# Cross attention with a fused output: output projection turned round, 512 columns moving

## The chip, the cores and the metric

The kernel runs on one core of a Trainium2 chip. The metric is the device time of one execution in microseconds; a change is judged by the times of several runs of the kernel before and the kernel after.

## What is computed

For each of 32 batches there are 512 tokens of 640 channels (x) and 77 context tokens of 1,024 channels, all fp32. What of the reference matters for the output (the object, others and ip branches take part with empty contexts, since there are just 77 context tokens, and add nothing):

```python
q = _heads(hidden_states @ to_q_w)                      # 20 heads of 32 channels
h_txt = _sdpa(q, _heads(ehs_txt @ to_k_w), _heads(ehs_txt @ to_v_w))
out = _merge(h_txt) + ...
out = out @ to_out_w + to_out_b
out = (out + residual) / RESCALE                        # residual = x, RESCALE = 1
```

## The kernel before

There are two stages. `project_context` makes keys and values of all context tokens (scratch in DRAM) and splits the weights into a high and a low fp32r part; it takes the first 325 us or so. `attend` then goes through the 32 batches and is the rest.

A batch has five steps g = 0 to 4, one for each group of four heads (128 channels). The order on each engine is written out by hand in the tables `TENSOR`, `SCALAR`, `VECTOR` and `POOL` (lines 67 to 86), one string for a step; the SyncE queue is written in its own body (lines 518 to 536). The letters:

- TensorE: S is the scores of the step (32 small matmuls, L750). Q0 to Q4 is the projection of q for the next step (15 matmuls of 512 columns, L735: five channel chunks, three products of high and low parts each). V is probabilities times values for the step two before (8 matmuls, L762). O and P are the output projection of the batch before and of the one before that (L776). Its unit is a half tile: 128 tokens by 320 channels, 15 matmuls with attention output o_t as weights and wo moving in 320 columns. There are eight a batch, k = 0 to 7.
- VectorE: M takes the maxima of the scores (L638), R the reciprocals of the sums (L644), T turns the probabilities (L654), Q copies q out of its bank (L661), W makes the low part of o_t (L665), Y turns x of the next batch (L671) and X makes its low part (L676). O and P add the output bank to the tile `x_bias` (L684).
- ScalarE: S0 to S3 are the exponentials (16 pairs of instructions, L595), X the high part of turned x (L608), V the high part of o_t (L602). D and E issue loads of x for turning (L582), R issues loads of x by rows into `x_bias` (L587).
- GpSimd: N normalises the probabilities (L562), C adds the bias to `x_bias` (L557).
- SyncE: in each step it loads v, reads back the turned probabilities of the step before from scratch (L508), stores finished output tiles (L496: one tile of 128 tokens, 320 KB, in rows of 2,560 B), and writes the turned probabilities of this step (L500). The load of k is in step 0.

x is turned in squares of 32 x 32: it is loaded in four quarters of 160 channels each, in runs of 640 B, and VectorE's transpose within 32 partitions does the rest. The channels of turned x thus come in a permuted order, and wq is loaded in the same order. Turned x (`x_turned`) has one buffer, the output bank `fill_bank` has two.

In the last batch there is no next x to turn and no q to project in step 4. What is left of the output projection (P5, P6, P7 of batch 30 and all eight of batch 31) stands behind the loop (lines 798 to 804), between and after the last two V.

Of the kernel before, what the change touches and what calls it, by code (L numbers as in the profile page):

```python
# [19 lines left out]
F32, F32R = mybir.dt.float32, mybir.dt.float32r  # L20
# [42 lines left out]
def orders(*steps):  # L63
# [3 lines left out]
TENSOR = orders("S Q0 Q1 Q2 Q3 Q4 P5 V",  # L67
# [4 lines left out]
SCALAR = orders("S0 S1 S2 S3 D1 V",  # L72
                "S0 S1 S2 S3 D2 D3 V",
                "S0 S1 S2 S3 R0 V",
                "S0 S1 S2 S3 R1 R2 X0 X1 X2 X3 X4 V",
                "S0 S1 S2 S3 R3 E0 V")
VECTOR = orders("M W R0 Q R1 T0 R2 T1 R3 T2 P5 T3",
# [30 lines left out]
def cross_attention(nc, x, ctx, wq, wk, wv, wo, bias, out):  # L108
# [3 lines left out]
    with ExitStack() as stack:  # L112
# [13 lines left out]
        x_rows = x.rearrange("b (t p) c -> b p t c", p=P)  # L126
        project_context(nc, ctx, wq, wk, wv, wo, kept, k_scratch, v_scratch, x_v, x_loaded)
        attend(nc, x_v, x_rows, bias, out, kept, k_scratch, v_scratch, p_scratch, x_loaded)


def project_context(nc, ctx, wq, wk, wv, wo, kept, k_scratch, v_scratch, x_v, x_loaded):

    with ExitStack() as stack:  # L133
# [29 lines left out]
        WK_CHUNKS, WKV_CHUNKS = KC, 2 * KC  # L163

# [135 lines left out]
        def _(dve):  # L300
            def split_weights(which):
                for n in which:
                    _, dst, k = chunks[n]
                    dve.wait_ge(w_high, n + 1)
                    nc.vector.tensor_tensor(dst[:, 1, k, :], stage[:, n % WSLOTS, :], dst[:, 0, k, :].bitcast(F32),  # L305
# [84 lines left out]
def attend(nc, x_v, x_rows, bias, out, kept, k_scratch, v_scratch, p_scratch, x_loaded):  # L390

    with ExitStack() as stack:
# [432 lines left out]
```

## Time and profile before

| | us |
|---|---|
| median of 3 runs | 1845.81 (1843.40 to 1849.78) |
| profiled execution, its own time | 1846.19 |
| its span | 1844.5 |
| TensorE busy in the span | 1796.0 (97%) |
| VectorE busy | 1167.8 (63%) |
| ScalarE busy | 1054.0 (57%) |
| GpSimd busy | 689.8 (37%) |
| the core's DMA engines, mean rate | 217 GB/s |

The profile is one execution. Busy time of an engine is the union of its instructions; weight loads of TensorE are counted by themselves. The granted clock of TensorE is given as a share of 2.4 GHz; its lower level is 1.2 GHz. In a timeline or in the chain, consecutive instructions of one line are merged, with their count behind an x; the figure in brackets is idle time before the first, with what ended it.

### The profile page before, as it was taken

How to read it: one execution, taken by the hardware profiler on the slowest of the kernel's cores; microseconds unless marked ns; L12 is line 12 of the kernel's file. 1: busy time of each engine (PE TensorE's matmuls, PEld its weight loads, DVE VectorE, ACT ScalarE, POOL GpSimd, SP SyncE). 2: the span in 40 equal slices, each digit the busy share in tenths (PEclk: the TensorE clock that was granted, in tenths of full speed). 3: DMA queues.
4: the chain of work that ended last, by engine and by line, in shares of the span. 5: the costliest groups of instructions: out<-in, count | busy, mean ns of one | idle time of the engine just before them, and what ended most of it. 6: DMA issues, size and time to landing. Idle time of an engine off the chain costs nothing.

```text
span 1844.5 us, 41902 instructions
## 1 busy us (share of the span) xinstructions
PE 1796.0 (97%) x14960; PEld 1508.3 (82%) x14960; DVE 1167.8 (63%) x2402; ACT 1054.0 (57%) x5597; POOL 689.8 (37%) x865
## 2 busy tenths in 40 slices
PE   8999998689999999999999999999999999999997
PEld 7999998468888888888888888888888888888886
DVE  3201010577777777777777777777777777777762
ACT  4312111476666666666666666666666666666661
POOL 1111111244444444444444444444444444444441
PEclk9999999799999999999999999999999999999998
DMA  7422110588989989989898998988989989998973
GB/s 264 136 85 86 63 44 33 143 227 250 252 247 247 252 249 250 249 250 252 246 251 251 249 250 247 253 248 248 250 251 249 250 249 251 246 254 246 253 217 125
DMA packets 271397, 399.36 MB, mean 217 GB/s; under 512 B 41088, under 2 KB 119024, under 8 KB 271200
## 3 DMA queue, kind: packets, MB, share of 16 engines
q1 hardware_dynamic: 183008, 301.62, 56.1%
q10 hardware_dynamic: 83904, 82.59, 18.5%
q0 software_dynamic: 4288, 12.62, 1.9%
q8 instruction: 111, 1.82, 0.4%
q14 instruction: 86, 0.70, 0.1%
HBM read 216.37 MB, written 180.39 MB: 215 GB/s over the span
## 4 chain that ended last, share of the span: by engine, by line
PE 78%; DVE 1%; ACT 1%; DMA 0%; POOL 0%; issue 0%; SPq 0%; ACTq 0%; DVEq 0%
PE p_bank L735 31%; PE p_bank L776 31%; PE p_scores L750 9%; PE p_bank L762 8%; ACT probs L595 1%; DVE negmax L638 0%; POOL probs L562 0%; DMA probs_t<-p_scratch 0%; DVE turned L654 0%; DMA p_scratch<-turned 0%; DVE x_raw L671 0%; DVE x_t L676 0%; DVE q_t L661 0%; DVE rsum L644 0%; DVE x_bias L684 0%
## 5 line engine op out<-in xcount | busy, mean ns | idle before, releaser
L595 ACT ACTIVATE probs<-p_scores,negmax 128x77 f32<-128x77 f32 x2560 | 787.8, 361 | 332.0 <-DVE negmax L638 332.0
L562 POOL TENSOR_TENSOR probs<-probs,rsum 128x308 f32<-128x308 f32 x640 | 446.5, 700 | 844.4 <-DVE rsum L644 844.3
L595 ACT ACTIVATION_READ_ACCUMULATOR probs<-p_scores,negmax 128x1 f32 x2560 | 622.1, 243 | 0.0
L735 PE MATMUL p_bank<-x_t,wq_split 128*128 128x512 f32 x2400 | 598.9, 401 | 15.8 <-DVE x_t L676 15.8
L776 PE MATMUL p_bank<-wo_split,o_t 128*128 128x320 f32 x3840 | 599.4, 310 | 0.6 <-DVE x_bias L684 0.6
L776 PEld LDWEIGHTS p_bank<-wo_split,o_t 128*128 128x128 f32 x3840 | 578.4, 189 | 17.4 <-issue 2.5
L735 PEld LDWEIGHTS p_bank<-x_t,wq_split 128*128 128x128 f32 x2400 | 445.1, 190 | 116.8 <-DVE x_t L676 17.0
L654 DVE STREAM_TRANSPOSE turned<-probs 128x384 f32<-128x384 f32 x640 | 356.8, 558 | 29.3 <-POOL probs L562 29.0
L638 DVE TENSOR_REDUCE negmax<-p_scores 128x16 f32<-128x1232 f32 x160 | 227.7, 1423 | 86.4 <-PE p_scores L750 86.4
L750 PEld LDWEIGHTS p_scores<-k_sb,q_t 32*128 32x128 f32 x5120 | 157.5, 186 | 146.9 <-issue 146.9
L644 DVE RECIPROCAL rsum<-sums 128x4 f32<-128x4 f32 x640 | 111.1, 174 | 187.6 <-ACT probs L595 183.3
L602 ACT ACTIVATE o_t<-p_bank 128x512 fp32r<-128x512 f32 x160 | 98.5, 615 | 180.7 <-PE p_bank L762 180.7
L557 POOL TENSOR_TENSOR x_bias<-x_bias,bias_all 128x640 f32<-128x640 f32 x128 | 196.4, 1555 | 0.0
L750 PE MATMUL p_scores<-k_sb,q_t 32*128 32x77 f32 x5120 | 181.0, 277 | 13.9 <-ACT probs L595 12.4
L762 PE MATMUL p_bank<-probs_t,v_sb 77*32 77x512 f32 x1280 | 171.3, 607 | 7.1 <-DMA probs_t<-p_scratch 7.1
L311 DVE TENSOR_TENSOR ctx_t<-p_bank,ctx_t 128x512 fp32r<-128x512 f32 (+1 forms) x40 | 26.9, 672 | 224.9 <-ACT ctx_t L264 224.9
L356 PE MATMUL p_bank<-ctx_t,wk_split 128*128 128x256 f32 (+1 forms) x1200 | 156.3, 288 | 2.2 <-DVE wk_split L305 2.2
L356 PEld LDWEIGHTS p_bank<-ctx_t,wk_split 128*128 128x128 f32 x1200 | 148.7, 194 | 2.9 <-DVE wk_split L305 2.6
L661 DVE COPY q_t<-p_bank 128x512 f32<-128x512 f32 x160 | 109.3, 683 | 61.3 <-PE p_bank L735 61.3
L671 DVE STREAM_TRANSPOSE x_raw<-x_raw 128x512 f32<-128x512 f32 x160 | 108.5, 680 | 54.8 <-PEq L133 54.0
L370 PE MATMUL p_bank<-wv_split,ctx_t 128*128 128x320 f32 (+1 forms) x960 | 142.4, 309 | 0.0
L370 PEld LDWEIGHTS p_bank<-wv_split,ctx_t 128*128 128x128 f32 (+1 forms) x960 | 139.0, 184 | 1.9 <-DVE wv_split L305 0.2
(28 smaller groups left out, 634.2 us busy)
## 6 DMA issues: line engine op xcount, KB each, us to landing
p_scratch<-turned SPq DMA_DIRECT2D x160, 768.0 KB, 6.8
probs_t<-p_scratch SPq DMA_DIRECT2D x320, 256.0 KB
x_bias<-in_x ACTq DMA_DIRECT2D x128, 320.0 KB, 3.5
out<-x_bias SPq DMA_DIRECT2D x128, 320.0 KB, 5.6
x_raw<-in_x ACTq DMA_DIRECT2D x124, 320.0 KB, 5.5
probs_t<-p_scratch SPq DMA_DIRECT2D x160, 104.0 KB
ctx_raw<-in_ctx SPq DMA_DIRECT2D x19, 512.0 KB, 4.6
k_sb<-k_scratch SPq DMA_DIRECT2D x32, 192.5 KB, 6.1
```

The source lines that it names most:

```text
L356: last = nc.tensor.matmul(k_bank[slot][:, 0:tokens], wk_s[:, a, k, m * P:(m + 1) * P], ctx_t[parity][:, b, k, 0:tokens], start=n == 0, sto ...
L370: last = nc.tensor.matmul(v_bank[u % 2][0:rows, 0:HALF], ctx_t[parity][:, a, k, t0:t0 + rows], wv_s[:, b, k, hf * HALF:(hf + 1) * HALF], s ...
L557: nc.gpsimd.tensor_tensor(x_bias[:, parity, t, :], x_bias[:, parity, t, :], bias_all[:, :], ALU.add).then_inc(x_bias_ready, 1)
L562: nc.gpsimd.tensor_tensor(heads_of(t), heads_of(t), rsum[:, slot, t, :].unsqueeze(2).to_broadcast([P, HG, N_TXT]), ALU.mult).then_inc(prob ...
L595: last = nc.scalar.activation(heads_of(t)[:, h, :], s_bank[:, h, t * N_TXT:(t + 1) * N_TXT], ACT.Exp, bias=negmax[:, slot, t, h:h + 1], ac ...
L638: nc.vector.tensor_reduce(negmax[:, slot, :, :], s_bank[:, :, 0:QT * N_TXT].rearrange("p h (t k) -> p t h k", k=N_TXT), AX.X, ALU.max, neg ...
L644: nc.vector.reciprocal(rsum[:, slot, t, :], sums[:, slot, t, :]).then_inc(rsum_ready, 1)
L654: nc.vector.transpose(turned[slot][:, :, :, t, :].rearrange("p k h q -> p h k q"), squares_of(t)).then_inc(probs_turned, 1)
L735: last = nc.tensor.matmul(q_bank[:, :], wq_s[:, w, c, g * P:(g + 1) * P], x_t[:, a, c, :], start=c == 0 and i == 0, stop=c == CC - 1 and i ...
L750: last = nc.tensor.matmul(s_bank[:, h, t * N_TXT:(t + 1) * N_TXT], q_t[slot][rows, t * P:(t + 1) * P], k_sb[parity][rows, g, :], start=Tru ...
L762: last = nc.tensor.matmul(pv_bank[h * HD:(h + 1) * HD, :], v_sb[:, g, h * HD:(h + 1) * HD], probs_t[slot][:, :, h, :], start=True, stop=True)
L776: last = nc.tensor.matmul(to_bank[:, 0:HALF], o_t[parity][:, o, c, t * P:(t + 1) * P], wo_s[:, w, c, hf * HALF:(hf + 1) * HALF], start=c = ...
```

## The change

- The output projection takes wo as weights and moves 512 columns of o_t. Its unit becomes a chunk of 128 output channels by all 512 tokens of the batch, 15 matmuls; there are five a batch, k = 0 to 4, one in each step. wo's output channels are put in the order of turned x (`staged`, `split_part`).
- The second loading of x (`x_bias`, L587) and the bias adds on GpSimd (L557) are gone. VectorE joins bank, turned x and the bias, now a column of one value for each partition, in one `scalar_tensor_tensor`, in place into turned x, which gets three buffers.
- VectorE turns each joined chunk back (`turn_output`, Z in the table: five a batch, in steps 0 to 2 two batches later) into `out_blocks`, which has one buffer.
- The output is stored by quarters of 160 channels, in runs of 640 B. All four stores of a batch wait for its five turns; in the loop two stand in step 2 and two in step 3.
- The bias is loaded by four small loads, values of 4 B, one for each 32 partitions.
- Loads and turns of x are a step earlier than before. Behind the loop stand P3 and P4 of batch 30, the five chunks of batch 31, and their adds and turns.

```diff
-TENSOR = orders("S Q0 Q1 Q2 Q3 Q4 P5 V",
-                "S Q0 Q1 Q2 Q3 Q4 P6 P7 V",
+TENSOR = orders("S Q0 Q1 Q2 Q3 Q4 P3 V",
+                "S Q0 Q1 Q2 Q3 Q4 P4 V",
                 "S Q0 Q1 Q2 Q3 Q4 O0 V",
-                "S Q0 Q1 Q2 Q3 Q4 O1 O2 V",
-                "S O3 Q0 Q1 Q2 Q3 Q4 O4 V")
-SCALAR = orders("S0 S1 S2 S3 D1 V",
-                "S0 S1 S2 S3 D2 D3 V",
-                "S0 S1 S2 S3 R0 V",
-                "S0 S1 S2 S3 R1 R2 X0 X1 X2 X3 X4 V",
-                "S0 S1 S2 S3 R3 E0 V")
-VECTOR = orders("M W R0 Q R1 T0 R2 T1 R3 T2 P5 T3",
-                "M W R0 Q R1 T0 R2 T1 R3 T2 P6 T3 P7",
-                "M W Y0 R0 Q R1 T0 R2 T1 Y1 R3 T2 O0 T3 Y2",
-                "M W Y3 R0 Q R1 T0 Y4 R2 T1 R3 T2 O1 T3 X0 X1 O2",
-                "M X2 X3 X4 W R0 R1 T0 O3 R2 T1 Q R3 T2 T3 O4")
-POOL = orders("N0 N1 N2 N3 C0 C1",
-              "N0 N1 N2 N3 C2 C3",
-              "N0 N1 N2 N3",
-              "N0 N1 N2 N3",
-              "N0 N1 N2 N3")
-
-HALVES = 2 * QT
-CREDIT = 16
+                "S Q0 Q1 Q2 Q3 Q4 O1 V",
+                "S O2 Q0 Q1 Q2 Q3 Q4 V")
+SCALAR = orders("S0 S1 S2 S3 D3 V",
+                "S0 S1 S2 S3 V",
+                "S0 S1 S2 S3 V",
+                "S0 S1 S2 S3 E0 X0 X1 X2 X3 X4 V",
+                "S0 S1 S2 S3 E1 E2 V")
+VECTOR = orders("M W Z0 R0 Q R1 T0 Z1 R2 T1 R3 T2 Z2 T3 P3",
+                "M W Z3 R0 Q R1 T0 Y0 R2 T1 R3 T2 Y1 T3 P4",
+                "M W Z4 R0 Q R1 T0 Y2 R2 T1 R3 T2 Y3 T3 O0",
+                "M W Y4 R0 Q R1 T0 R2 T1 R3 T2 T3 X0 X1 O1",
+                "M X2 X3 X4 W R0 R1 T0 O2 R2 T1 Q R3 T2 T3")
+POOL = orders(*["N0 N1 N2 N3"] * CC)
+
+XT = 3
...
+        def staged(n):
+
+            chunk = stage[:, n % WSLOTS, :]
+            return chunk.rearrange("p (i k s) -> p k i s", i=P // SQ, s=SQ) if chunks[n][0] is wo else chunk
+
+        def split_part(n, part):
+
+            dram, dst, k = chunks[n]
+            chunk = dst[:, part, k, :]
+            return chunk.rearrange("p (k i s) -> p k i s", i=P // SQ, s=SQ) if dram is wo else chunk
...
-                    _, dst, k = chunks[n]
                     act.wait_ge(w_loaded[n % WSLOTS], DMA * loads_by(n))
-                    nc.scalar.activation(dst[:, 0, k, :], stage[:, n % WSLOTS, :], ACT.Copy).then_inc(w_high, 1)
+                    nc.scalar.activation(split_part(n, 0), staged(n), ACT.Copy).then_inc(w_high, 1)
...
-        bias_all = sbuf("bias_all", [P, C])
+        bias_t = sbuf("bias_t", [P, CC])
         x_blocks = x_raw[:, 0, :, :]
-        x_turned = x_raw[:, 1, :, :].rearrange("p n c -> p (n c)").rearrange("p (c s) -> p c s", s=S)
-        x_bias = sbuf("x_bias", [P, 2, QT, C])
+        x_turned = [x_raw[:, 1, :, :].rearrange("p n c -> p (n c)").rearrange("p (c s) -> p c s", s=S)]
+        x_turned += [sbuf(f"x_turned{i}", [P, CC, S]) for i in range(1, XT)]
+        out_blocks = sbuf("out_blocks", [P, S // SQ, CQ])
...
-            def store_out(b, parity, t):
-                sp.wait_ge(out_added, HALVES * b + 2 * t + 2 + CREDIT)
-                sp.dma_start(out_v[b][t], x_bias[:, parity, t, :]).then_inc(out_stored[t], DMA)
+            def store_out(b, i):
+                sp.wait_ge(out_turned, CC * (b + 1))
+                sp.dma_start(out_v[b][i], out_blocks[i * SQ:(i + 1) * SQ, :, :]).then_inc(out_stored, DMA)
 
             def write_probs(n, slot):
                 sp.wait_ge(probs_turned, QT * (n + 1))
@@ -509,8 +510,10 @@
                                  p_scratch[slot, k].rearrange("(i p) c -> p i c", p=SQ)[0:rows])\
                       .then_inc(probs_read[slot], DMA)
 
-            sp.dma_start(bias_all[:, :], bias.rearrange("(a n) -> a n", a=1).broadcast_to([P, C]))\
-              .then_inc(bias_loaded, DMA)
+            for i in range(P // SQ):
+                sp.dma_start(bias_t[i * SQ:(i + 1) * SQ, :], bias.rearrange("(i k s) -> i s k", i=P // SQ, s=SQ)[i],
+                             allow_slow_non_contiguous=True)\
+                  .then_inc(bias_loaded, DMA)
...
-                    for kind, k in TENSOR[(g - 1) % CC]:
-                        if kind == "O" and k % 2 == 1 and g > 0 and age > 0:
-                            store_out(b - 1, 1 - parity, k // 2)
-                        if kind == "O" and k % 2 == 1 and g == 0 and age > 1 or kind == "P" and k % 2 == 1 and age > 1:
-                            store_out(b - 2, parity, k // 2)
+                    if g in (2, 3) and age > 1:
+                        store_out(b - 2, 2 * g - 4)
+                        store_out(b - 2, 2 * g - 3)
...
-            store_out(B - 2, (B - 2) % 2, 1)
             sp.wait_ge(pv_done, CC * B - 2)
             read_probs(CC * B - 1, (CC * B - 1) % 2)
-            for t in (2, 3):
-                store_out(B - 2, (B - 2) % 2, t)
-            for t in range(QT):
-                store_out(B - 1, (B - 1) % 2, t)
-            for t in range(QT):
-                sp.wait_ge(out_stored[t], DMA * B)
+            for b in (B - 2, B - 1):
+                for i in range(P // SQ):
+                    store_out(b, i)
+            sp.wait_ge(out_stored, DMA * (P // SQ) * B)
...
-            pool.wait_ge(bias_loaded, DMA)
-
-            def add_bias(b, parity, t):
-
-                pool.wait_ge(x_bias_loaded[t], DMA * (b + 1))
-                nc.gpsimd.tensor_tensor(x_bias[:, parity, t, :], x_bias[:, parity, t, :], bias_all[:, :],
-                                        ALU.add).then_inc(x_bias_ready, 1)
...
-            def load_x_bias(b, parity, t):
-                if b > 1:
-                    act.wait_ge(out_stored[t], DMA * (b - 1))
-                act.dma_start(x_bias[:, parity, t, :], x_rows[b][:, t, :]).then_inc(x_bias_loaded[t], DMA)
...
-                nc.vector.transpose(x_turned[:, c, :].rearrange("p (n q) -> p n q", q=SQ),
+                nc.vector.transpose(x_turned[b % XT][:, c, :].rearrange("p (n q) -> p n q", q=SQ),
...
-            def add_output(b, k, parity, from_bank):
-                t, hf = k // 2, k % 2
-                dve.wait_ge(out_done, HALVES * b + k + 1)
-                dve.wait_ge(x_bias_ready, QT * b + t + 1)
-                tile = x_bias[:, parity, t, hf * HALF:(hf + 1) * HALF]
-                nc.vector.tensor_tensor(tile, from_bank[:, 0:HALF], tile, ALU.add).then_inc(out_added, 1)
-
-            dve.sem_inc(out_added, CREDIT)
+            def add_output(b, k):
+                n = CC * b + k
+                if n == 0:
+                    dve.wait_ge(bias_loaded, DMA * (P // SQ))
+                dve.wait_ge(out_done, n + 1)
+                tile = x_turned[b % XT][:, k, :]
+                nc.vector.scalar_tensor_tensor(tile, fill_bank[n % 2][:, :], bias_t[:, k:k + 1], tile,
+                                               ALU.add, ALU.add).then_inc(out_added, 1)
+
+            def turn_output(b, k):
+                dve.wait_ge(out_added, CC * b + k + 1)
+                if b > 0:
+                    dve.wait_ge(out_stored, DMA * (P // SQ) * b)
+                nc.vector.transpose(out_blocks[:, :, k * SQ:(k + 1) * SQ],
+                                    x_turned[b % XT][:, k, :].rearrange("p (n q) -> p n q", q=SQ))\
+                  .then_inc(out_turned, 1)
...
-            add_output(B - 2, 5, (B - 2) % 2, fill_bank[1])
+            for k in range(3):
+                turn_output(B - 2, k)
+            add_output(B - 2, 3)
+            turn_output(B - 2, 3)
             ot_low_part(B - 1, CC - 2, (B - 1) % 2)
-            for k in (6, 7):
-                add_output(B - 2, k, (B - 2) % 2, fill_bank[k % 2])
+            add_output(B - 2, 4)
+            turn_output(B - 2, 4)
             ot_low_part(B - 1, CC - 1, (B - 1) % 2)
-            for k in range(HALVES):
-                add_output(B - 1, k, (B - 1) % 2, fill_bank[k % 2])
+            for k in range(CC):
+                add_output(B - 1, k)
+                turn_output(B - 1, k)
...
-            def project_out(b, k, parity, to_bank):
-                if k >= 2:
-                    pe.wait_ge(out_added, HALVES * b + k - 1 + CREDIT)
-                else:
-                    pe.wait_ge(out_added, HALVES * b + CREDIT)
-                t, hf = k // 2, k % 2
+            def project_out(b, k, parity):
+                n = CC * b + k
+                if n >= 2:
+                    pe.wait_ge(out_added, n - 1)
                 for c in range(CC):
                     if k == 0 and c in (0, CC - 1):
                         pe.wait_ge(ot_ready, CC * b + (CC - 1 if c == 0 else CC))
                     for i, (o, w) in enumerate(PASSES):
-                        last = nc.tensor.matmul(to_bank[:, 0:HALF], o_t[parity][:, o, c, t * P:(t + 1) * P],
-                                                wo_s[:, w, c, hf * HALF:(hf + 1) * HALF],
-                                                start=c == 0 and i == 0, stop=c == CC - 1 and i == 2)
+                        last = nc.tensor.matmul(fill_bank[n % 2][:, :], wo_s[:, w, c, k * P:(k + 1) * P],
+                                                o_t[parity][:, o, c, :], start=c == 0 and i == 0,
+                                                stop=c == CC - 1 and i == 2)
...
-            project_out(B - 2, 5, (B - 2) % 2, fill_bank[1])
+            project_out(B - 2, 3, (B - 2) % 2)
             sum_values(B - 1, CC - 1, (CC * B - 1) % 2)
-            for k in (6, 7):
-                project_out(B - 2, k, (B - 2) % 2, fill_bank[k % 2])
-            for k in range(HALVES):
-                project_out(B - 1, k, (B - 1) % 2, fill_bank[k % 2])
+            project_out(B - 2, 4, (B - 2) % 2)
+            for k in range(CC):
+                project_out(B - 1, k, (B - 1) % 2)
```

## Rows read from the trace of the kernel before

**Rows 1.** Window: us, busy (instructions) of PE, PEld, DVE, ACT, POOL; clock, DMA share, GB/s.
```profile
700.00:1700.00 1000.00, 1000.00 (x8588) 811.08 (x8587) 758.24 (x1581) 661.53 (x3687) 435.77 (x522) 1.00 0.90 250
```

**Rows 2.** Chain of waits, steady batches: start us, us, what. Step 4, then parts of steps 0 and 1.
```profile
415.13 1.06 PE p_scores L750 x32
416.19 2.39 PE p_bank L776 x15
418.58 3.43 PE p_bank L735 x15
422.01 2.20 PE p_bank L776 x15
424.21 1.00 PE p_bank L762 x8
...
426.26 3.63 PE p_bank L735 x15
...
437.78 4.40 PE p_bank L776 x30
```

**Rows 3.** Groups of instructions by line, middle stretch: busy us, mean ns | idle before.
```profile
L671 DVE STREAM_TRANSPOSE x_raw<-x_raw 128x512 f32<-128x512 f32 x109 | 74.2, 680 | 0.0
```

**Rows 4.** Timelines of TensorE and of VectorE in one batch: start us, us, what [idle before].
```profile
1207.80 1.13 PE L750 MATMUL p_scores<-k_sb,q_t 32*128 32x77 f32 x32
...
1212.41 2.36 PE L776 MATMUL p_bank<-wo_split,o_t 128*128 128x320 f32 x15
...
1203.83 0.58 DVE L654 STREAM_TRANSPOSE turned<-probs 128x384 f32<-128x384 f32 x1 [0.50 <-POOL probs L562]
...
1205.25 0.65 DVE L661 COPY q_t<-p_bank 128x512 f32<-128x512 f32 x1
...
1209.00 1.44 DVE L638 TENSOR_REDUCE negmax<-p_scores 128x16 f32<-128x1232 f32 x1 [1.25 <-PE p_scores L750]
...
1212.61 0.69 DVE L661 COPY q_t<-p_bank 128x512 f32<-128x512 f32 x1 [0.59 <-PE p_bank L735]
...
1235.60 1.40 DVE L638 TENSOR_REDUCE negmax<-p_scores 128x16 f32<-128x1232 f32 x1
...
1243.08 0.58 DVE L654 STREAM_TRANSPOSE turned<-probs 128x384 f32<-128x384 f32 x1
...
1244.75 0.48 DVE L684 TENSOR_TENSOR x_bias<-p_bank,x_bias 128x320 f32<-128x320 f32 x1
1245.15 1.43 DVE L638 TENSOR_REDUCE negmax<-p_scores 128x16 f32<-128x1232 f32 x1
...
1248.30 0.69 DVE L665 TENSOR_TENSOR o_t<-p_bank,o_t 128x512 fp32r<-128x512 f32 x1
1248.90 0.48 DVE L644 RECIPROCAL rsum<-sums 128x4 f32<-128x4 f32 x2
1249.88 0.58 DVE L654 STREAM_TRANSPOSE turned<-probs 128x384 f32<-128x384 f32 x1 [0.50 <-POOL probs L562]
```

**Rows 5.** Timelines of VectorE and TensorE at the start of the second stage.
```profile
336.34 0.69 DVE L661 COPY q_t<-p_bank 128x512 f32<-128x512 f32 x1 [4.00 <-PE p_bank L735]
...
337.13 1.13 PE L750 MATMUL p_scores<-k_sb,q_t 32*128 32x77 f32 x32 [0.83 <-issue]
```

**Rows 6.** The end of the program: TensorE's timeline, the chain of waits, a window.
```profile
1807.77 1.93 PE L762 MATMUL p_bank<-probs_t,v_sb 77*32 77x512 f32 x8 [4.80 <-DMA probs_t<-p_scratch]
1809.63 4.25 PE L776 MATMUL p_bank<-wo_split,o_t 128*128 128x320 f32 x15
...
1816.73 6.14 PE p_bank L776 x30
...
1841.35 0.49 DVE x_bias L684
...
1807.00:1816.00 9.00, 6.45 (x27) 4.38 (x31) 1.09 (x2) 0.60 (x1) 3.91 (x3) 0.63 0.71 233
```

**Rows 7.** ScalarE's queue at the start of the second stage: four loads of x issued.
```profile
329.40 2.02 ACTq L582 DMA_DIRECT2D x_raw<-in_x  x4
```

More of the change, by code:

```diff
@@ L125, in cross_attention @@
         x_v = x.rearrange("b (n q) (i c) -> b i q n c", q=SQ, i=P // SQ)
-        x_rows = x.rearrange("b (t p) c -> b p t c", p=P)
+        out_v = out.rearrange("b (n q) (i c) -> b i q n c", q=SQ, i=P // SQ)
         project_context(nc, ctx, wq, wk, wv, wo, kept, k_scratch, v_scratch, x_v, x_loaded)
-        attend(nc, x_v, x_rows, bias, out, kept, k_scratch, v_scratch, p_scratch, x_loaded)
+        attend(nc, x_v, bias, out_v, kept, k_scratch, v_scratch, p_scratch, x_loaded)
 def project_context(nc, ctx, wq, wk, wv, wo, kept, k_scratch, v_scratch, x_v, x_loaded):
@@ L302, in split_weights @@
                 for n in which:
-                    _, dst, k = chunks[n]
                     dve.wait_ge(w_high, n + 1)
-                    nc.vector.tensor_tensor(dst[:, 1, k, :], stage[:, n % WSLOTS, :], dst[:, 0, k, :].bitcast(F32),
+                    nc.vector.tensor_tensor(split_part(n, 1), staged(n), split_part(n, 0).bitcast(F32),
                                             ALU.subtract).then_inc(w_split, 1)
@@ L387, in _, with attend @@
             blocks(pe, body)
-def attend(nc, x_v, x_rows, bias, out, kept, k_scratch, v_scratch, p_scratch, x_loaded):
+def attend(nc, x_v, bias, out_v, kept, k_scratch, v_scratch, p_scratch, x_loaded):
     with ExitStack() as stack:
@@ L430, in attend @@
         xt_turned, xt_high, xt_ready = sem("xt_turned"), sem("xt_high"), sem("xt_ready")
-        out_done, out_added = sem("out_done"), sem("out_added")
-        x_bias_ready = sem("x_bias_ready")
-        x_bias_loaded = [sem(f"x_bias_loaded{t}") for t in range(QT)]
-        out_stored = [sem(f"out_stored{t}") for t in range(QT)]
-        out_v = out.rearrange("b (t p) c -> b t p c", p=P)
+        out_done, out_added, out_turned, out_stored = (sem("out_done"), sem("out_added"), sem("out_turned"),
+                                                       sem("out_stored"))
         def heads_of(t):
@@ L465, in steps @@
                 for kind, k in order[g]:
-                    left_out = (kind in "OC" and age == 0 or kind == "P" and age < 2 or kind in "XY" and last
+                    left_out = (kind == "O" and age == 0 or kind in "PZ" and age < 2 or kind in "XY" and last
                                 or kind == "V" and age == 0 and g < 2 or kind == "W" and age == 0 and g < 3
@@ L567, in body @@
                 for g, slot, kind, k in steps(POOL, b, parity, age, last):
-                    if kind == "N":
-                        normalise(b, g, slot, k)
-                    elif kind == "C":
-                        add_bias(b - 1, 1 - parity, k)
+                    normalise(b, g, slot, k)
             batches(body)
-            for t in range(QT):
-                add_bias(B - 1, (B - 1) % 2, t)
         @block.scalar
@@ L607, in xt_high_part @@
                     act.wait_ge(q_done, CC * b)
-                nc.scalar.activation(x_t[:, 0, c, :], x_turned[:, c, :], ACT.Copy).then_inc(xt_high, 1)
+                nc.scalar.activation(x_t[:, 0, c, :], x_turned[b % XT][:, c, :], ACT.Copy).then_inc(xt_high, 1)
             for c in range(CC):
@@ L622, in body @@
                         xt_high_part(b + 1, k)
-                    elif kind == "R":
-                        load_x_bias(b, parity, k)
                     elif kind == "D" and 0 < b < B - 1:
```

12 lines of the change are left out of this document (7 added, 5 removed).

## The prediction

> **What bounds the kernel now.** I read the busy time by stretch first: over 1,000 us in the middle TensorE is busy for all 1,000, at the full granted clock of 2.4 GHz, VectorE for 758, ScalarE for 662 [rows 1]. Then the chain of waits shows what that means in time: in the middle it is nothing but blocks of matmuls, end to end [rows 2]. So a batch costs what its blocks cost, and VectorE, ScalarE, GpSimd and the transfers matter only if one of them becomes late.
>
> The blocks [rows 2]: scores (S) 1.06, query projection (Q) 3.63 behind scores and 3.43 behind a projection, one half tile of the output projection (O) 2.20, or 2.39 behind scores, two of them 4.40, values (V) 1.00. A batch is 5 x 1.06 + 4 x 3.63 + 3.43 + 7 x 2.20 + 2.39 + 5 x 1.00 = 46.04 us. Its five steps are uneven: with one O 7.89 us, with two 10.09 or 10.08.
>
> **The change part by part.**
>
> *Output matmuls.* Removed are 120 matmuls of 320 columns per batch (2.20 / 15 = 147 ns each), added are 75 of 512 columns. The columns are the same 38,400. The new form has exactly the shape of the Q matmul (128x128 weights, 512 moving columns of the same type), which costs 3.43 / 15 = 229 ns. So an output chunk costs 3.43, and 3.63 directly behind scores, as Q does. There are five a batch, one a step, of which one is behind scores (step 4: S O2 Q V): 4 x 3.43 + 3.63 = 17.35 in place of 7 x 2.20 + 2.39 = 17.79. Gain 0.44 us a batch; new batch 45.6, and every step 9.12. The gain is only the share per matmul that is not columns; bounds from the same rows: nothing, if the new block ran at the per-column price of the old (0.458 ns x 512 x 15 = 3.52, sum 17.8), and 0.44.
> The Trainium skill (TensorE: Matmul & The Clock Gate, Back-to-back issue gap) gives columns / 2.4 plus about 2.5 ns per matmul. By it 45 fewer matmuls would be worth only 0.11 us a batch, an estimate from that page. The trace disagrees at both sizes, 147 ns against its 136 and 229 against its 216, and the measurement decides.
>
> *How much of it arrives.* Batches 2 to 30 are full: 29 x 0.44 = 12.8. In batch 1 only steps 2 to 4 hold output work: 27.4 for 28.1, gain 0.7. In batch 31 the next landmark is the scores of step 3, after steps with one, two and one O: 25.9 before, 3 x 9.12 = 27.4 after, loss 1.5. At that landmark the new kernel is 12.0 us ahead.
>
> *Does VectorE keep up?* Per batch it loses 8 adds of 320 (0.40 from start to start) and gains 5 joined adds of 512 and 5 transposes back. The trace has no scalar_tensor_tensor. Nearest is the subtraction from PSUM of 512 elements, 0.60 from start to start; I take that, since it too reads one PSUM and one SBUF operand. Bounds: 0.40 (the 320 add) and 1.4, the maxima over 1232 elements [rows 4]. The transposes back I take as those of x, 0.68 [rows 3], 0.67 from start to start. VectorE gains 5 x 0.60 + 5 x 0.67 - 3.2 = 3.2 us a batch, on 46.04 x 0.758 = 34.9 busy; it ends at about 38 of 45.6. The cover is its idle time, but position matters. In steps 0 to 2 the work behind the last probs transpose ends at about 10.1 after the step's scores start, and the next maxima can start at 9.12 + 1.20 = 10.32: fits. The tight place is step 3 to 4, in the terms of [rows 4] (all counted from a step's scores): maxima start at 1.20; last transpose T3 7.48 later (1235.60 to 1243.08), 8.68; then X0, X1 and the add take 2.07 until the next maxima, 0.20 more with 512 elements: 10.95, that is 1.83 in step 4. From the maxima to T0 4.73 (1245.15 to 1249.88): 6.56. From T0 to the copy of q 1.42 (1203.83 to 1205.25) and 0.20 more: VectorE is there at 8.18. The block Q now ends at 1.06 + 3.63 + 3.43 = 8.12, since O4 no longer stands behind it, and the copy starts 0.20 after (1212.41 to 1212.61): 8.32. The copy takes 0.69 and the scores start 0.10 after it, as at the start of the stage (copy 336.34 + 0.69, scores 337.13 [rows 5]): 9.11, where V ends at 9.12. So no stall, with a reserve of 0.15 us on VectorE's side and none on the copy's. Queued behind that wait are the scores of the next batch's step 0, and all that follows on TensorE. I take 0 and keep 0.3 a batch (9 us) in the range.
>
> *Exponentials.* A step must leave room for maxima, 16 exponentials and the release of the scores' banks. That fits in 7.89 today with TensorE never idle [rows 1]; the new steps are 9.12, and the maxima of step 4, 0.6 late, use half of the new room. Nothing.
>
> *GpSimd and ScalarE.* The bias adds (1.55 us each on GpSimd) and the second loading of x leave; both lay beside the matmuls. Worth 0. The last load of x moves from step 1 to step 0 and the turns of x from step 2 to step 1, so their distance stays. Worth 0.
>
> *Transfers.* 1.3 MB a batch is no longer read; the 1.3 MB stored go in runs of 640 B instead of 2,560. On SyncE two stores now stand in steps 2 and 3 between the read-back of probs and the next write of probs: at some 0.45 us each they finish about when T3 does, delaying that write by 0.1; V uses it two steps later. Worth 0. The single out_blocks buffer makes the first turn back wait for the stores of the batch before, which were issued three steps earlier. Worth 0.
>
> *Start.* Four bias loads stand ahead of k on SyncE instead of one: 3 x 0.4 = 1.2 us later, and k is wanted only at 337.13. Their 4-byte runs have no row; between 0 and 3 us, I take 0.3, because the q copy ends last there today. (The Trainium skill, DMA: Bandwidth & Descriptors, head table, asks for 512 B and more per run for full rate. No row here shows runs so short, and the bias is 640 of them, once.)
>
> *End.* V of step 3 in the last batch starts a fixed time after that step's scores [rows 6], so it is 12.0 early. From there (1807.77) to the last matmul's end (1841.3) it was 33.55. After: V 1.86 (the granted clock is 0.63 on average from 1807 to 1816, after 4.8 us idle); chunk 3 at the lower clock 4.25 x 512 / 320 = 6.8, or less if the clock returns inside it; then V of step 4 waits for a subtraction that stands on VectorE behind the add and the new turn: 0.68 + 0.67 + 0.68, 2.1 with the handovers; V 1.06; six chunks 20.6, and 1.7 for clock again, what the first two halves lost today (6.14 against 4.40). Sum 34.1, so 0.5 lost; bounds -3 and +3. Then today one add (0.49) and one store of 320 KB: 3.2 from the last matmul to the span's end. After: add 0.68, turn 0.67, and all four stores of the batch, since the quarters cut across channels and wait for the last turn. Issuing four takes 2.0 [rows 7], landing 2.3 more, or about 5.5 if 1.3 MB flows at the 250 GB/s of the middle: 5.6 to 7.2, I take 6.5, 3.3 more than today.
>
> **Sum.** -12.0 + 0.5 + 3.3 + 0.3 = -7.9. The profiled execution took 1846.2 (span 1844.5), the median is 1845.8: 1846.2 - 7.9 - 0.4 = 1838.
>
> **The rivals.**
> *A: the copy of q becomes late* (step 4). For it: two new long adds and three x subtractions stand on that path, with 0.15 us to spare; against: VectorE has 7 us of slack a batch. With adds of 0.75 from start to start the path is 0.3 longer, the stall 0.15 to 0.3, a loss of 5 to 9: about 1845, no change.
> *B: slower.* The same place, with the joined add much longer than the subtraction (the extra per-partition operand), or the transposes back slower than those of x: a stall of 0.26 us a batch (adds of 0.81) uses up the 7.9, and from 0.43 (adds of 0.89) the kernel is measurably slower than today. At 1.1 us both adds lengthen the path by 1.0, the stall is 0.85 x 30 = 25, time 1863; the other bound, 1.4, would cost more. Against: each 512-element kind in the trace costs 0.68 or less.
> *C: hardly any gain in the matmuls*, if the new block costs its columns at the old price (3.52) or o_t moves slower than x does: then the end decides, and the time is 1838 + 0.44 x 30 = 1851, or 1845 at half of it. The Q rows speak against it. (The page named above would put it there: 0.11 a batch makes about 1848.)
> *D: the end goes well and nothing stalls*, the clock returns early in the first chunk of the tail and the stores land in 5 us: 1834.
>
> **How the numbers follow.** A comparison of this kernel can tell some 0.3%, 5.5 us: faster means below 1840.3, slower above 1851.3. Forecast 45% and D 12%, both faster for nearly all their width; A 23%, C 8%, both same; B 12%. Some of the forecast's width reaches above 1840.3. Faster 0.54, same 0.33, slower 0.13. The range 1832 to 1849 leaves out B and the far ends.
>
> **What would show it.** In the chain: blocks of 3.43 for the output, steps of 9.12, a batch of 45.6; scores of step 0 with no wait for the copy of q (a wait there is A). VectorE: joined add near 0.68, with B from 0.95. In the tail: V of step 4 released by VectorE, not by a transfer, and 6.5 us from the last matmul to the end. A batch above 46.0 or TensorE idle in the middle would make the forecast wrong.

## The result: slower by 0.8%

| | before | after |
|---|---|---|
| median, us (5 runs each) | 1844.56 (1843.40 to 1849.78) | 1859.48 (1859.31 to 1861.81) |
| ratio, 95% interval | | 1.0081 (1.0070 to 1.0093) |
| profiled execution, its span | 1846.19, 1844.5 | 1859.48, 1857.8 |
| TensorE / VectorE / GpSimd busy | 97 / 63 / 37% | 97 / 68 / 27% |
| weight loads busy | 82% | 74% |

The forecast was 1838 in a range to 1849. The time lies 21 us above it, on the other side of the kernel before.

The window of the middle stretch answers to [rows 1], with the same columns: TensorE is as full as before, at the full clock (1.00). No wait took the place of the work removed.

```profile
700.00:1700.00 1000.00, 999.98 (x7559) 723.00 (x7559) 818.45 (x1620) 658.82 (x3671) 302.58 (x434) 1.00 0.84 219
```

The chain of waits answers to [rows 2]. In order: scores of step 0 of batch 2; step 4 and the start of step 0 in the middle; scores of step 0 of batch 31. L729 is the query projection, L768 the output projection.

```profile
424.94 1.12 PE p_scores L744 x32
...
925.24 1.06 PE p_scores L744 x32
926.30 3.69 PE p_bank L768 x15
929.99 3.50 PE p_bank L729 x15
933.49 0.99 PE p_bank L756 x8
934.48 1.12 PE p_scores L744 x32
935.60 3.69 PE p_bank L729 x15
939.29 3.50 PE p_bank L768 x15
...
1768.18 1.12 PE p_scores L744 x32
```

From the first of these rows to the last are 29 batches in 1343.24 us, 46.32 each; before they took 46.04, and 45.60 was forecast. The output block takes 3.49 (3.69 behind scores) where 3.43 was forecast. The surprise is the query block, which the change does not touch in any line: 3.70 behind scores and 3.50 behind the output block, where it took 3.63 and 3.43 in [rows 2]. All 512-column matmuls are some 4 ns slower each.

The new instructions of VectorE by line (busy us, mean ns | idle before), and the stretch before the critical copy of q (the last row). The joined add is longer than the 0.68 taken, 0.72, and 0.63 to 0.66 from start to start.

```profile
L664 DVE SCALAR_TENSOR_TENSOR x_turned<-p_bank,bias_t,x_turned 128x512 f32<-128x512 f32 x70 | 50.1, 716 | 0.0
L671 DVE STREAM_TRANSPOSE out_blocks<-x_turned 128x512 f32<-128x512 f32 x70 | 48.2, 689 | 0.0
```

```profile
1018.92 0.74 DVE L664 SCALAR_TENSOR_TENSOR x_turned<-p_bank,bias_t,x_turned 128x512 f32<-128x512 f32 x1
...
1024.81 0.71 DVE L664 SCALAR_TENSOR_TENSOR x_turned<-p_bank,bias_t,x_turned 128x512 f32<-128x512 f32 x1
1025.44 0.16 DVE L623 RECIPROCAL rsum<-sums 128x4 f32<-128x4 f32 x1
...
1026.13 0.69 DVE L640 COPY q_t<-p_bank 128x512 f32<-128x512 f32 x1
```

TensorE in the same place, the block Q, the values and the scores of step 0:

```profile
1022.44 3.65 PE L729 MATMUL p_bank<-x_t,wq_split 128*128 128x512 f32 x15
1026.02 1.06 PE L756 MATMUL p_bank<-probs_t,v_sb 77*32 77x512 f32 x8
1027.08 1.13 PE L744 MATMUL p_scores<-k_sb,q_t 32*128 32x77 f32 x32
```

Over the middle stretch this copy starts 0.43 us after the last of its matmuls starts, as the other four copies of a batch do, which all wait for theirs. So it is the block Q that releases it here, and VectorE is there some 0.1 sooner. From the copy's end (1026.82) to the scores are 0.26, where 0.10 was taken, so the scores of step 0 start 1.06 after V, and those of the other steps 1.00.

The end answers to [rows 6]: the scores of step 3 in the chain; TensorE's timeline with both last V, the chunk between them and the last output chunks; VectorE's first turn of the last batch, which waited 5.51 for the stores of the batch before, and its last; then the transfers of the last 9 us (from 1849 to 1858, in 40 slices).

```profile
1795.99 1.11 PE p_scores L744 x32
...
1815.45 1.94 PE L756 MATMUL p_bank<-probs_t,v_sb 77*32 77x512 f32 x8 [4.44 <-DMA probs_t<-p_scratch]
1817.31 4.92 PE L768 MATMUL p_bank<-o_t,wo_split 128*128 128x512 f32 x15
...
1824.44 1.06 PE L756 MATMUL p_bank<-probs_t,v_sb 77*32 77x512 f32 x8 [2.21 <-DVE o_t L644]
...
1840.41 7.26 PE L768 MATMUL p_bank<-o_t,wo_split 128*128 128x512 f32 x30 [0.70 <-DVE x_turned L664]
...
1839.01 0.71 DVE L671 STREAM_TRANSPOSE out_blocks<-x_turned 128x512 f32<-128x512 f32 x1 [5.51 <-DMA out<-out_blocks]
...
1848.50 0.71 DVE L671 STREAM_TRANSPOSE out_blocks<-x_turned 128x512 f32<-128x512 f32 x1
...
GB/s 0 0 0 0 23 188 182 185 188 185 182 182 185 182 182 179 185 174 188 145 171 256 290 259 216 233 196 202 196 185 179 182 179 185 131 31 0 0 0 0
DMA packets 2112, 1.31 MB, mean 146 GB/s; under 512 B 64, under 2 KB 2112, under 8 KB 2112
```

The account in the profiled executions, after minus before, counted to four landmarks: scores of step 3 in batch 31 +9.8 (1786.23 before, 1795.99; forecast -12.0); from there to V of step 3 -2.1 (21.54 before, 19.46; forecast 0); to the last matmul's end -1.3 (33.55 before, 32.2; forecast +0.5); to the end of the span +6.9 (3.2 before, 10.1; forecast +3.3). Sum +13.3, the difference of the spans. The forecast names 0.3 more for the start of the stage. So practically the whole miss is in the first term; the three of the end add up to +3.5, where +3.8 was forecast.

### The profile page after: what moved, and what is told of

The parts are those of the page before. It is cut to its first block, busy times and chain, and to the rows that moved or that the text cites. A ratio compares the mean times of both kernels' runs of the same rounds, so it can differ in the third digit from the quotient of the medians.

```text
span 1857.8 us, 38728 instructions
## 1 busy us (share of the span) xinstructions
PE 1801.6 (97%) x13520; PEld 1381.6 (74%) x13520; DVE 1261.6 (68%) x2466; ACT 1054.8 (57%) x5597; POOL 497.5 (27%) x737
## 4 chain that ended last, share of the span: by engine, by line
PE 78%; DVE 2%; ACT 1%; DMA 1%; POOL 0%; issue 0%; SPq 0%; ACTq 0%; DVEq 0%
PE p_bank L729 31%; PE p_bank L768 30%; PE p_scores L744 9%; PE p_bank L756 8%; ACT probs L576 1%; DVE negmax L617 0%; DMA out<-out_blocks 0%; DVE turned L633 0%; POOL probs L553 0%; DMA p_scratch<-turned 0%; DMA probs_t<-p_scratch 0%; DVE x_t L655 0%; DVE x_raw L650 0%; DVE out_blocks L671 0%; SPq L497 0%
## 5 line engine op out<-in xcount | busy, mean ns | idle before, releaser
L729 PE MATMUL p_bank<-x_t,wq_split 128*128 128x512 f32 x2400 | 607.1, 405 | 15.5 <-DVE x_t L655 15.5
L768 PE MATMUL p_bank<-o_t,wo_split 128*128 128x512 f32 x2400 | 589.7, 397 | 0.7 <-DVE x_turned L664 0.7
L729 PEld LDWEIGHTS p_bank<-x_t,wq_split 128*128 128x128 f32 x2400 | 445.6, 190 | 126.1 <-DVE x_t L655 16.4
L768 PEld LDWEIGHTS p_bank<-o_t,wo_split 128*128 128x128 f32 x2400 | 449.0, 188 | 112.5 <-issue 2.5
L633 DVE STREAM_TRANSPOSE turned<-probs 128x384 f32<-128x384 f32 x640 | 352.5, 551 | 40.0 <-POOL probs L553 39.8
L644 DVE TENSOR_TENSOR o_t<-p_bank,o_t 128x512 fp32r<-128x512 f32 x160 | 108.9, 680 | 0.0
L287 ACT ACTIVATE v_out<-p_bank 128x320 f32<-128x320 f32 (+1 forms) x40 | 17.5, 438 | 122.6 <-PE p_bank L374 119.4
```

Of the source, the lines that this page charges most:

```text
L633: nc.vector.transpose(turned[slot][:, :, :, t, :].rearrange("p k h q -> p h k q"), squares_of(t)).then_inc(probs_turned, 1)
L644: nc.vector.tensor_tensor(o_t[parity][:, 1, g, :], pv_bank[:, :], o_t[parity][:, 0, g, :].bitcast(F32), ALU.subtract).then_inc(ot_ready, 1)
L729: last = nc.tensor.matmul(q_bank[:, :], wq_s[:, w, c, g * P:(g + 1) * P], x_t[:, a, c, :], start=c == 0 and i == 0, stop=c == CC - 1 and i ...
L768: last = nc.tensor.matmul(fill_bank[n % 2][:, :], wo_s[:, w, c, k * P:(k + 1) * P], o_t[parity][:, o, c, :], start=c == 0 and i == 0, stop ...
```

## The experiments

Two numbers decide in most of them. One is the mean time from start to start of the matmuls inside a block (the first of the 14 times of a block left out, 700 to 1,700 us, worked out from the start times in each trace). The other is where the tiles lie in a partition, which follows from the order and sizes of the allocations, each rounded up to 32 B. wq starts at 37,504 and wo at 63,104 in all but two kernels; both leave 128 on division by 512, as do all slices of them that a matmul loads. "Distance" is the rest of the moving tile minus that of the weights, modulo 512. The kernel before was run again with every round (medians 1844.73 to 1846.74), and ratios are to that; where it says one run, there is no interval, but each mean of the 512-column blocks is over some 1,400 matmuls even so.

| kernel | query: distance, ns | output, 512 columns: distance, ns | batch, us |
|---|---|---|---|
| before | 0, 229.5 | (320 columns) 146.4 | 46.04 |
| after | 32, 233.2 | 96, 233.7 | 46.32 |
| a_pad, a_order, a_tail | 64, 229.4 to 229.5 | 128, 232.3 | 45.99 |
| t_swapps, t_swapw | 64, 229.4 | 128, 232.2 to 232.3 | 45.99 |
| a_o64 | 64, 229.8 | 192, 232.9 | 46.07 |
| a_noturn | 32, 233.1 | 96, 233.7 | 46.31 |
| t_swapsb | 128, 232.5 | 64, 229.6 | 45.98 |
| t_low, t_hi0, t_all64 | 0, 228.0 to 228.2 | 0, 227.0 | 45.62 to 45.64 |
| t_best | 0, 228.1 | 0, 227.0 | 45.48 |
| t_mix | 64, 229.2 | 256, 228.3 | 45.74 |
| b_qorder | 0, 229.5 | (320) 146.4 | 46.04 |
| b_shift32 | 32, 233.2 | (320) 146.9 | 46.37 |
| b_shift64 | 64, 229.3 | (320) 146.5 | 46.10 |
| b_high | 64, 229.6 | (320) 146.7 | 46.11 |

**First round: the tiles' places against VectorE's traffic.** The unchanged query block had slowed, so either where x_t lies or what runs beside it had to be the cause. The new bias tile is 20 B per partition and pushes x_t and o_t 32 B off a 64 B boundary.

a_pad:
```diff
-        bias_t = sbuf("bias_t", [P, CC])
+        bias_t = sbuf("bias_t", [P, 16])
```


> The changed kernel with its bias tile widened from 5 to 16 floats per partition (64 B in place of 20), nothing else. In the changed kernel every tile allocated behind the bias, x_t and o_t among them, starts 32 B off a 64 B boundary; here all start on one. Theory 1 (placement): the 512-column matmuls go from 233 ns start to start to 229, a block from 3.50 to 3.43, a batch from 46.3 to 45.6 us, the time from 1859 to about 1838. Theory 2 (VectorE's added reads and writes of SBUF slow TensorE's reads): nothing changes, 1859.

```profile
1308.61 3.64 PE p_bank L729 x15
1312.25 3.48 PE p_bank L768 x15
```

Measured 1850.70 (ratio to before 1.0025, 1.0015 to 1.0034). In the chain (query, output) the query block is back at 3.64, the output block hardly moved: 3.48. Half of the steady loss is gone, the time that theory 1 named is missed by 13 us.

b_shift32, an unused tile behind the bias of the kernel before:
```diff
         bias_all = sbuf("bias_all", [P, C])
+        shift = sbuf("shift", [P, 8])
```


> The kernel before with an unused tile of 32 B per partition behind the bias, so that x_t, o_t and all later tiles start 32 B off a 64 B boundary; wq and wo stay where they were. Theory 1: the query projection, which moves x_t, goes from 229 to 233 ns a matmul, a batch from 46.04 to about 46.4, the time up by 10 us to about 1855; the output projection, which moves wo, stays at 147 if only the moving operand counts. Theory 2: nothing changes, 1845.

```profile
1307.23 3.69 PE p_bank L736 x15
1310.92 2.21 PE p_bank L777 x15
```

Measured 1856.93 (1.0057, 1.0041 to 1.0074), query block 3.69 where it was 3.63, with no other work than before. 32 B of nothing cost 10 us. The output block, where o_t is loaded as weights, stays at 2.21.

b_shift64, the same with `[P, 16]`:

> The kernel before with an unused tile of 64 B per partition at the same place: everything moves, but stays on 64 B boundaries. Theory 1: all as before, query projection 229 ns a matmul, 1845. If it slows here too, it is not the boundary but the distance between tiles. Theory 2: 1845.

One run, 1849.13; query matmuls 229.3. As theory 1 has it, except that the batch is 0.06 longer.

a_noturn, `out_blocks` filled by full transposes in batch 0 only:
```diff
-                nc.vector.transpose(out_blocks[:, :, k * SQ:(k + 1) * SQ],
+                n = S // SQ if b == 0 else 1
+                nc.vector.transpose(out_blocks[:, 0:n, k * SQ:(k + 1) * SQ],
```


> The changed kernel, with the turning back of the output cut to one 32-column square of each chunk from batch 1 on (most of the output is left unturned), waits and order kept. Theory 1: matmuls stay at 233 ns and a batch at 46.3; the time falls only at the end, by 1 to 2 us. Theory 2: VectorE moves about 3 us less a batch, the matmuls fall towards 229 ns, the time by up to 20 us.

```profile
1314.22 3.70 PE p_bank L730 x15
1317.92 3.49 PE p_bank L769 x15
```

One run, 1856.66: both blocks as in the changed kernel, with 2.3 us a batch less busy time on VectorE. Theory 2 falls.

**Second round: why output matmuls stay at 232, and the end.** a_order (in `project_out`, on a_pad):
```diff
-                    for i, (o, w) in enumerate(PASSES):
+                    for i, (w, o) in enumerate(PASSES):
```


> The changed kernel with the 64 B bias tile, and in the output projection the three products of a channel chunk in the order high-high, then wo low with o_t high, then wo high with o_t low: the moving plane stays the same for two matmuls running, as it does in the query projection. With the 64 B tile alone the query block is back at 3.64 but the output block only at 3.48, 232 ns a matmul. Theory 1 (the order of the planes is what is left): output matmuls at 229 to 230, block 3.44, a batch 0.2 us less, 1845. Theory 2 (it is where o_t or wo lies, or that o_t is used at all): unchanged at 232 and 1851.

1851.24 (1.0021, 1.0012 to 1.0031), 232.3 ns: unchanged, the theory falls.

a_o64 (on a_pad, `shift = sbuf("shift", [P, 16])` ahead of o_t):

> The changed kernel with the 64 B bias tile and another 64 B of nothing ahead of o_t, so that o_t leaves the 128 B boundary on which wo also starts and has the offset that x_t has. If the place of o_t within 128 B matters, the output matmuls fall from 232 to 229; if the order of the planes or the tensor itself is the cause, they stay at 232 and the time near 1851.

One run, 1852.30, 232.9 ns: the rest modulo 128 is not it.

b_qorder, the same exchange of loop variables in `project_q` of the kernel before:

> The kernel before with the products of the query projection in the other order, so that the moving plane of x_t changes at nearly every matmul, as o_t's does in the changed kernel. Order theory: query matmuls from 229.5 to about 232, a batch up by 0.2 us, 1851. Place theory: nothing moves, 1845.

One run, 1846.32; 229.5 ns as before. The order of the planes plays no part.

a_tail, on a_pad:
```diff
+                to = x_blocks if b == B - 1 else out_blocks   # no wait for out_stored in the last batch
...
+            ot_low_part(B - 1, CC - 2, (B - 1) % 2)
             add_output(B - 2, 3)
             turn_output(B - 2, 3)
-            ot_low_part(B - 1, CC - 2, (B - 1) % 2)
...
+        PARTS = ((0, 3), (3, CC))                              # stores of the last batch; i = 2, 3 by ScalarE
+            eng.wait_ge(out_turned, CC * (B - 1) + k1)
```


> The changed kernel with the 64 B bias tile and another end: the last batch is turned into the idle half of x_raw instead of waiting for out_blocks, it is stored in two parts (chunks 0 to 2, then 3 and 4), half of the stores issued by ScalarE's queue, and the subtraction that the last V waits for stands ahead of the add and turn of chunk 3. In the kernel with the 64 B tile alone the last matmul ends 35.0 us after V of step 3 starts and the span 10.0 after that. If the end is lost to the store rate and to VectorE's order: 31 to 32 and 6 to 7, the time from 1851 to about 1844. If the stores of 256-byte runs are no faster than those of 640, only the first part is gained: 1847.

```profile
1806.74 1.94 PE L769 MATMUL p_bank<-probs_t,v_sb 77*32 77x512 f32 x8 [4.75 <-DMA probs_t<-p_scratch]
...
1814.39 1.06 PE L769 MATMUL p_bank<-probs_t,v_sb 77*32 77x512 f32 x8 [0.98 <-DMA probs_t<-p_scratch]
...
1837.37 0.71 DVE x_raw L684
```

Measured 1844.29 (0.9987, 0.9977 to 0.9996), 6 to 7 us under a_pad. In TensorE's timeline both last V wait for their transfers and no longer for VectorE; from V of step 3 to the last matmul 29.8 us (35.0 in a_pad), and from there to the span's end (1842.2) 5.6 (10.0). Part of the 35.0 is clock: from 1800 to 1842 the granted clock was 0.84 in the profiled a_pad, 0.92 in the changed kernel and 0.91 here. Against the 32.2 and 10.1 of the changed kernel the new end gives 2.4 and 4.5. These are VectorE's order and the stores; the edits were made together, and no run takes them apart.

The stores of the last batch, from 1830 to 1842.2 in 40 slices, chunks 0 to 2 first, then 3 and 4:

```profile
GB/s 0 0 0 0 0 0 64 172 259 264 277 315 310 281 312 277 47 0 0 0 0 0 0 0 0 0 0 0 0 92 149 241 276 284 229 270 173 5 0 0
DMA packets 4224, 1.31 MB, mean 107 GB/s; under 512 B 4224, under 2 KB 4224, under 8 KB 4224
```

These runs are shorter (384 and 256 B for 640), and the rate is higher, 230 to 315 GB/s for about 185. So it was not the length of the runs that held the rate in the changed kernel.

**Third round: exchange of places**, all on a_tail. t_swapsb allocates o_t where x_t is and x_t where o_t is; t_swapps exchanges the PSUM banks; t_swapw exchanges wq and wo.

> The kernel with the 64 B bias tile and the new end, with o_t allocated in the place of x_t and x_t in the place of o_t. There the query matmuls took 229.4 ns start to start and the output matmuls 232.3. Theory place (high in the partition is slower to read): the two change over, output 229 to 230, query 232. Theory other (banks, weights, or the writers of the tile): they stay as they are.

```profile
1309.93 3.69 PE p_bank L742 x15
1313.62 3.44 PE p_bank L781 x15
```

> The same kernel as a base, with the PSUM banks of query and output projection exchanged (query in the fourth bank, output in the first and third). If the bank written to makes the difference, the output matmuls on the first bank fall to 229 and the query rises to 232; otherwise nothing moves: 229.4 and 232.3, 1844.

> The same kernel as a base, with the places of wq and wo exchanged. If the place of the weights makes the difference, query 232 and output 229; otherwise 229.4 and 232.3, 1844.

One run each: 1843.46, 1842.80, 1843.73. In the first the two kinds change over: query 3.69, output 3.44 (in the chain's rows), 232.5 and 229.6 ns. Exchanging the banks (229.4 and 232.2) or the weights (229.4 and 232.3) does nothing. It is the place of the moving tile; the weights' exchange leaves both at the same rest modulo 512, so it says nothing yet of the distance to them.

**Fourth round: which places.** t_low, on a_tail:
```diff
+        x_t = sbuf("x_t", [P, 2, CC, S], F32R)
+        o_t = [sbuf(f"o_t{i}", [P, 2, CC, S], F32R) for i in range(2)]
         bias_t = sbuf("bias_t", [P, 16])
```


> The kernel with the 64 B bias tile and the new end, with x_t and both o_t allocated first, below 150,144 B of the partition, everything else behind them. Exchanging x_t and o_t exchanged their speeds (232.5 and 229.6 ns). Place theory: both at 229.5 now, a batch from 45.99 to about 45.8, the time from 1844 to about 1838, 0.4% under the kernel before. If only one certain place is fast and not the lower part as such, one of them stays at 232 and the time near 1844.

```profile
1311.01 3.62 PE p_bank L742 x15
1314.64 3.40 PE p_bank L781 x15
...
1336.20 0.99 PE p_bank L769 x8
1337.19 0.15 issue
1337.34 1.13 PE p_scores L757 x32
```

1833.22 (0.9931, 0.9917 to 0.9944), better than its own theory: 227 and 228 ns. Both blocks are under the forecast (3.62 and 3.40). The last three rows show what came with it: V, then 0.15 of waiting, then the scores of step 0.

b_high, x_t allocated last in the kernel before:

> The kernel before, x_t allocated last, from 196,800 B of the partition, on a 64 B boundary as before; o_t, which is loaded as weights here, 20,480 B lower. Place theory: query matmuls from 229.5 to 232.5, a batch 0.22 us longer, 1852. If the effect needs the changed kernel's work around it: 1845.

One run, 1848.08, 229.6 ns. High and no slower: "the lower part is fast" falls. What all kernels up to here fit is the distance.

t_hi0 (on a_tail, padded so that x_t at 119,936 and o_t at 184,960 have distance 0), t_mix (on t_low, x_t 64 B and o_t 256 B off), t_all64 (on t_low, weights and moving tiles all 64 B up):

> The kernel with the 64 B bias tile and the new end, x_t and o_t left in their high places (119,936 and 184,960 B) but padded so that their addresses and those of wq and wo leave the same rest (128) on division by 512. With x_t and o_t first the matmuls took 228.0 and 227.0; there the rests are equal too. Theory distance (what counts is the difference of moving tile and weights modulo 512 B: 0 gives 227, 64 gives 229.5, 128 gives 232.3, off 64 B boundaries 233 and more): both kinds 227 to 229, a batch 45.6. Theory low place: the output matmuls stay at 232, a batch at 46.0.

```profile
1303.34 3.62 PE p_bank L743 x15
1306.97 3.40 PE p_bank L782 x15
```

> x_t and o_t first, as in the kernel with both in the low place, but x_t 64 B further and o_t 256 B further than the weights' rest modulo 512. Theory distance: query matmuls back at 229.5 although x_t is low; output matmuls off 227, at a value not yet seen (a distance of 256 B). Theory low place: both stay at 227 to 228.

> x_t and o_t first, and wq, wo, x_t and o_t all 64 B further up, so that each has the rest 192 modulo 512. If the difference between moving tile and weights counts: 227 to 228 as without the shift. If the address of the moving tile by itself counts: 229.5.

One run each. t_hi0, 1833.26: high places, 228.0 and 227.0 ns. t_mix, 1834.63: low places, 229.2 and 228.3. t_all64, 1831.88: other addresses, same distance, 228.2 and 227.0. Three for three for the distance. t_all64 also shows that it is a distance and not the moving tile's own address: x_t has the rest 192 there as in a_pad, 228.2 ns against 229.5, and the weights have moved with it.

t_best, on t_low:
```diff
-                "M X2 X3 X4 W R0 R1 T0 O2 R2 T1 Q R3 T2 T3"
+                "M X2 X3 X4 W R0 R1 T0 R2 T1 Q R3 T2 T3 O2"
```


> x_t and o_t first, and VectorE's joined add of step 4 (O2) moved behind the last probabilities, off the path to the copy of q. With x_t and o_t first a step is 9.08 us and the scores of step 0 wait 0.15 us for that copy in each batch. If the copy is late by VectorE's order: the wait goes, a batch from 45.62 to 45.4, the time from 1833 to 1828 or 1829. If it is late because the block Q ends late: nothing changes, 1833.

```profile
1331.98 1.00 PE p_bank L769 x8
1332.98 1.12 PE p_scores L757 x32
1334.10 3.63 PE p_bank L742 x15
1337.73 3.40 PE p_bank L781 x15
```

1827.33 (0.9906, 0.9889 to 0.9922). From the first to the second row, V to scores of step 0, are 1.00 us, where t_low has 1.14. This version is 0.9% faster than the kernel before and 32 us faster than the change as it was made.

## Why the prediction was wrong

**The step that failed is the first, the price of the output matmul.** It said: "The new form has exactly the shape of the Q matmul", so a chunk costs 3.43. The shape was right and not enough: the price also hangs on where the moving tile lies relative to the weights. The new bias tile moved x_t from distance 0 to 32; o_t, moving for the first time, lies at 96. Each query matmul is 3.7 ns dearer than before, and each output matmul costs 4.2 ns more than the 229.5 of the query matmul before. In the chain's rows the five query blocks of a batch are 0.35 us over the forecast (4 x 3.70 + 3.50 for 4 x 3.63 + 3.43), the five output blocks 0.34 (3.49 to 3.51 for 3.43, 3.69 for 3.63), and the wait below is 0.06. Together that is, but for rounding, the 0.72 between 46.32 and 45.60, and 29 batches of it are the 21 us. b_shift32 shows the query part by itself in the kernel before, and t_low, t_hi0 and t_all64 show that with distance 0 the block is 3.40, better than forecast. The premise that the query block stays at 3.63 was not even weighed; no rival had it. Rival C named the possibility that o_t moves slower than x_t, at 8%, but took the query block as fixed.

**The gain per batch was there to be had.** In t_best a batch is 45.48 for the 45.60 forecast, 0.56 under the kernel before. By the rows the output blocks are 0.57 of it (4 x 3.40 + 3.62 = 17.22 for 17.79) and the query blocks 0.07; the wait at step 0 takes 0.07 back. For the output blocks 0.44 was forecast, from fewer matmuls of the same columns; the other 0.13 is the lower price of 227.0 ns, which no one had forecast.

**The copy of q** (step 4): taken as no stall, with 0.15 us in hand on VectorE's side and none on the copy's. In the changed kernel that is nearly how it went. Counted from the scores of step 4, VectorE is ready for the copy at about 8.23 (8.18 forecast; its turn before starts at 7.76, and 0.47 after such a turn starts the next instruction can) and the copy starts at 8.36, released by its matmuls (8.32 forecast). What the forecast had wrong is the way from there to the scores: copy 0.69 and 0.26 more, not 0.10. V to scores of step 0 is on average 0.06 longer than in the other steps. With the faster blocks of t_low it is 0.22; there VectorE is the late one, since the copy starts 0.62 after its last matmul starts and directly behind a turn of probabilities. Moving O2 brings the copy back to 0.43 and the wait to 0.07, which is what the copy itself leaves. Rival B, an add long enough to turn the sign, is out: 0.72 us.

**The end** came out as forecast in sum (+3.5 for +3.8), and that is luck: its terms were off in both directions. V of step 3 came 2.1 earlier after its scores, where a fixed time was taken: its write of probabilities landed 5.0 us after the issue for 5.8 before, and the read-back took 5.1 for 6.3. The chunk behind that V was priced at 6.8 and took 4.86. V of step 4 waited for the subtraction, 2.21, about as forecast (2.1). Chunk 3 of the last batch waited 0.70 for an add queued behind the turn that waited for the stores; I had not priced that. The mis-sized term is the stores. I took 5.2 us from the last turn (turned at 1849.2) to the span's end; it was 8.6. Issuing the four took 4.0 where I had taken 2.0 from [rows 7], and the 1.31 MB moved at about 185 GB/s in most slices of that window (146 on average of it), where I had reckoned with 250. What held the rate is not shown. a_tail moved as much in shorter runs at 230 to 315 GB/s, issued by two queues, so the 640 B are not the reason; that there was one queue, or that it read 32 partitions at a time, remains possible. a_tail took back 6 to 7 us of all this.

**Right as forecast**: no other engine became the bound, GpSimd, transfers and the exponentials cost nothing, and the four bias loads cost nothing that can be seen (first scores at 336.79, 337.13 before).

**Open.** Seven distances were tried (0, 32, 64, 96, 128, 192, 256), each with these tiles only. The means hide something: the last four start-to-start times of a block are 226.7 ns at distance 0 in every kernel, the kernel before too, and also at distance 256. What differs is how long a block takes to settle: in the kernel before nine times at 225 to 236 and then four at 227, in t_low four at 229 to 233 and then 227. Why that is longer in the kernel before, and so its mean 229.5 and not 228, is open. Since 0 and 256 settle alike, the runs do not say whether the rest modulo 512 or modulo 256 counts, nor what in the chip makes the distance count.

## What to carry to other kernels

When a change adds, drops or resizes a tile, everything allocated behind it moves; look whether matmuls that the change does not touch have changed their price, and pad before judging the change. Give the moving tile and the weights of a long stream of fp32r matmuls the same address modulo 512 B. A 64 B boundary alone was worth little here: 128 and 192 cost 232.3 and 232.9 ns, 32 cost 233.2. And when a store buffer is cut across the order in which results come, price the end of the program by itself: everything that is stored after the last result is paid in full.

## What the runs showed of the hardware

- fp32r matmuls of 128 x 128 weights and 512 moving columns, at the full clock, mean start to start by distance modulo 512 B: 0: 227.0 (output), 228.0 to 228.2 (query), 229.5 (query, kernel before); 256: 228.3; 64: 229.2 to 229.8; 128: 232.3 to 232.5; 192: 232.9; 32: 233.1 to 233.2; 96: 233.7. The PSUM bank (t_swapps), the order of the products (a_order, b_qorder) and 2.3 us a batch less on VectorE (a_noturn) made no difference, and at distance 0 neither did the place in the partition (t_low, t_hi0).
- The last four times of a block: 226.7 at distance 0 and 256, 228.7 to 229.2 at 64, 232.4 to 233.7 at 128, 192, 32 and 96.
- Four stores of 320 KB from 32 partitions each, 640 B runs, one queue: about 185 GB/s, 4.0 us to issue. The same bytes in runs of 384 and 256 B over two queues: 230 to 315 GB/s (a_tail).
- o_t as weights, 32 B further: 146.9 for 146.4 ns at 320 columns.
- scalar_tensor_tensor, 128x512, from PSUM and SBUF with a scalar per partition: 0.72 us, against 0.68 for the plain subtraction [rows 4].
